# State-space B and C rows: from selection matmuls into PSUM to DMA out of DRAM into an SBUF ring

## The chip, the core and the metric

The kernel runs on one NeuronCore of one Trainium2 chip. The metric is the device time of one launch in microseconds (us). The names of the engines are those of the profile: PE is TensorE, DVE is VectorE, ACT is ScalarE, POOL is GpSimd, SP is the engine that issues the DMAs.

## What is computed

The network has six layers on 4 sequences of 512 tokens and 128 features, each with normalisation and a residual: a routed feed-forward attention ("ffn"), a 16-head attention ("mha"), the ffn again, a mixture of experts ("moe"), a state-space block ("mamba"), and the moe again. The change touches only the state-space block. Its core in the reference is

```python
x_dbl = x @ W_x                      # 96 columns: 64 for dt, 16 for B, 16 for C
dt = softplus(x_dbl[..., :64] @ W_dt + b_dt)
Bm = x_dbl[..., 64:80]
Cm = x_dbl[..., 80:]
def step(h, inp):
    dA = exp(dt_t[..., None] * A)
    h = dA * h + (dt_t * x_t)[..., None] * B_t[:, None, :]
    y = einsum('bdn,bn->bd', h, C_t)
```

with 256 inner channels d, 16 states n, 512 steps t. For each state n the recurrence over t is one scan for every channel. B and C depend on n and t and not on the channel, so the same row of 512 numbers is needed on all 128 partitions.

## The kernel before

**Units.** The program loops twice (`Fori(0, PAIRS)`) over two sequences at a time. In a pass the five engines walk through 12 units, `UNITS`: each layer for sequence 0 and then for sequence 1. So the state-space unit runs four times, twice in each pass. Every engine has its own instruction stream written out by hand, with explicit semaphore waits; nothing reorders it. While an engine works through a unit it also takes pieces ("stages") of the next unit's normalisation and routing, by the tables `DVE_STAGES`, `POOL_STAGES`, `ACT_STAGES` and `PE_STAGES` (L72 to L76), through `hand_over`, after the state with that number.

**Ahead of the states.** PE forms x_dbl for 512 tokens in PSUM bank 4, rows 0 to 63 for dt, rows 64 to 95 for B and C (L1513). ACT copies the dt rows (L815) and the B and C rows as bf16 (L816). DVE and POOL split the remainder into two more bf16 parts (L1158 to L1162 and L609), so that `n_bc` has the B and C rows three times, in 96 partitions, with a sum that is exact to float32. In the meantime PE, ACT, DVE and POOL compute dt as a guarded softplus on tiles of 128x1024 (two halves of the channels), L1167 to L1178 on DVE with L613 and L615 on POOL beside it.

**The loop over the states.** Per state n, for the two halves m of the channels:

- PE spreads row n of B over 128 partitions into bank 4 or 5 with one bf16 matmul against a selection matrix `pick` (L1527), and row n of C into bank 0 or 1 (L1531).
- ACT forms `n_da` = exp(dt * A) for each half (L831) and copies the C bank to SBUF, `n_cs` (L835).
- DVE multiplies dt*x by the B bank, `n_db` (L1186, one input in SBUF, one in PSUM), twice, and then runs the two scans `n_h` (L1194, both inputs in SBUF).
- POOL multiplies `n_h` by `n_cs` into `n_hc` (L623, both inputs in SBUF), twice.
- PE adds `n_hc` to the output in banks 2 and 3 by a float32 matmul against the identity (L1536).

`n_db`, `n_da`, `n_h` and `n_hc` exist once per half, so: the product of state n+1 waits for the scan of state n of its half, the scan of n+1 waits for POOL's product of n, and POOL's product of n+1 waits for PE.

```python
n_dbs.by(V.tensor_tensor(n_db[:, m, :], n_dtx[:, m, :], bank[:, 4 + n % 2, :], ALU.mult))
n_scan.by(V.tensor_tensor_scan(n_h[:, m, :], n_da[:, m, :], n_db[:, m, :], 0.0, ALU.mult, ALU.add))
n_hcs.by(nc.gpsimd.tensor_tensor(n_hc[:, m, :], n_h[:, m, :], n_cs[:, n // 2 % 2, :], ALU.mult))
```

After the last state DVE adds the skip term (L1202), gates (L1204), PE multiplies by W_out (L1542, 8 calls) and DVE adds the residual (L991).

**SP's stream** has the loads at the start, the expert weights, the attention's transfers over DRAM (`stack_dram`, `max_dram`), and the input and output of the pass. In the state-space units it has nothing to do.

## Time and profile before

| | |
|---|---|
| Time, median of 3 runs (us) | 1673.01 |
| Lowest and highest (us) | 1671.74, 1675.35 |
| Span of the profiled execution (us) | 1673.0 |
| PE busy | 1308.8 us, 78% |
| DVE busy | 1126.0 us, 67% |
| ACT busy | 685.1 us, 41% |
| POOL busy | 493.3 us, 29% |
| DMA moved | 33.11 MB, mean 20 GB/s |

The span is that of one execution taken by the profiler; it agrees with the median of the other runs within 0.1 us. Busy times are means over stages with different limits; the four state-space units lie at 522 to 636, 636 to 751, 1345 to 1458 and 1458 to 1573 us of the span. In a timeline, an instruction that the engine has begun but that cannot go on counts as busy. Two equal instructions that follow each other are merged, "x2". A float32 matmul shows as two records.

### The profile page before, as it was taken

To read this page: it belongs to the slowest core of one execution; us is meant where nothing else is said; L and a number is where in the kernel's file an instruction comes from. 1 tells how busy PE (TensorE), PEld (TensorE's weight loads), DVE (VectorE), ACT (ScalarE), POOL (GpSimd) and SP (SyncE) were. 2 spreads that over 40 slices of the span, in tenths; PEclk is the share of its full clock that TensorE was granted. 3 is DMA by queue.
4 is the path that set the end of the run, shared out by engine and by line. 5 is a ranking of instruction groups with operands and counts; after the bars stand their busy time and mean duration, and the time that the engine had idled before them with its cause. 6 is when DMAs were issued, how large, how long until landed. Compare 5 with 4: busy or idle time off the path is not lost.

```text
span 1673.0 us, 17199 instructions
## 1 busy us (share of the span) xinstructions
PE 1308.8 (78%) x5912; PEld 799.2 (48%) x5912; DVE 1126.0 (67%) x1997; ACT 685.1 (41%) x1136; POOL 493.3 (29%) x349
## 2 busy tenths in 40 slices
PE   0997768898977575669969967679988957747698
PEld 0675334576654122227636744336766622212366
DVE  5666655445775997987646665545556769889765
ACT  4443434343435344424425415253444443344244
POOL 2001000000644573646410010000016536547365
PEclk9998979899998677869979979799999977877899
DMA  5203030000000000000002020200000000000000
GB/s 204 57 14 88 4 89 3 1 1 1 1 1 0 1 0 0 1 1 1 13 33 70 19 71 22 70 3 1 1 1 1 1 0 1 0 1 0 1 1 19
DMA packets 23401, 33.11 MB, mean 20 GB/s; under 512 B 2992, under 2 KB 19152, under 8 KB 22864
## 3 DMA queue, kind: packets, MB, share of 16 engines
q1 hardware_dynamic: 23312, 31.99, 6.6%
q8 instruction: 48, 0.79, 0.2%
q14 instruction: 41, 0.34, 0.1%
HBM read 24.44 MB, written 8.06 MB: 19 GB/s over the span
## 4 chain that ended last, share of the span: by engine, by line
PE 47%; DVE 31%; issue 9%; DMA 5%; ACT 5%; POOL 1%; SPq 1%; POOLq 0%; DVEq 0%; ACTq 0%
PE bank L1227 10%; PE bank L1229 10%; PE bank L1228 10%; DVE n_h L1194 6%; DVE n_db L1186 4%; DVE a_mx L1132 3%; PE bank L1300 3%; PE bank L1236 2%; PE bank L1446 2%; DMA X<-in_x_dram 2%; PE bank L1486 2%; PE bank L1354 2%; DMA a_k<-stack_dram 2%; PE bank L1427 2%; DVE m_t L1057 1%
## 5 line engine op out<-in xcount | busy, mean ns | idle before, releaser
L590 POOL TENSOR_TENSOR m_hhl<-m_h,m_hhh 128x512 fp32r<-128x512 f32 x144 | 186.3, 1297 | 272.0 <-ACT m_hhh L755 271.7
L1536 PE MATMUL bank<-n_hc,ident 128*128 128x512 f32 x256 | 191.5, 861 | 83.1 <-POOL n_hc L623 79.8
L623 POOL TENSOR_TENSOR n_hc<-n_h,n_cs 128x512 f32<-128x512 f32 x128 | 210.4, 1662 | 128.9 <-DVE n_h L1194 123.7
L997 DVE SCALAR_TENSOR_TENSOR f_hl<-bank,f_hh 128x512 fp32r<-128x512 f32 x192 | 132.1, 690 | 128.1 <-ACT f_hh L695 127.0
L566 POOL TENSOR_TENSOR small<-small,half 128x4 f32<-128x4 f32 x24 | 24.3, 1012 | 600.3 <-DVE small L900 599.2
L695 ACT ACTIVATE f_hh<-bank 128x512 fp32r<-128x512 f32 x192 | 114.7, 597 | 207.1 <-PE bank L1300 206.7
L1194 DVE TENSOR_TENSOR_SCAN n_h<-n_da,n_db 128x512 f32<-128x512 f32 x128 | 192.0, 1538 | 3.4 <-POOL n_hc L623 2.3
L831 ACT ACTIVATE n_da<-n_dt,amat 128x512 f32<-128x512 f32 x128 | 91.7, 721 | 187.4 <-DVE n_h L1194 167.5
L1057 DVE TENSOR_TENSOR m_t<-m_sl,bank 128x512 f32<-128x512 f32 x128 | 87.8, 686 | 96.0 <-PE bank L1229 82.1
L1536 PEld LDWEIGHTS bank<-n_hc,ident 128*128 128x128 f32 x256 | 52.8, 241 | 187.0 <-POOL n_hc L623 177.1
L1132 DVE TENSOR_REDUCE a_mx<-bank 128x1 f32<-128x384 f32 (+3 forms) x176 | 105.9, 639 | 47.5 <-PE bank L1488 46.5
L1227 PE MATMUL bank<-xT_h,mw_h 128*128 128x512 f32 x288 | 123.7, 429 | 17.6 <-DVE m_t L1057 13.2
L749 ACT ACTIVATE m_sl<-bank 128x512 f32<-128x512 f32 x144 | 85.7, 596 | 120.4 <-PE bank L1229 118.3
L770 ACT ACTIVATE a_p<-bank 128x1024 f32<-128x1024 f32 (+3 forms) x128 | 86.9, 700 | 97.5 <-PE bank L1429 96.3
L755 ACT ACTIVATE m_hhh<-m_h 128x512 fp32r<-128x512 f32 x144 | 90.3, 627 | 68.0 <-DVE m_h L1060 48.8
L1228 PE MATMUL bank<-xT_l,mw_h 128*128 128x512 f32 x288 | 117.3, 407 | 0.0
L1229 PE MATMUL bank<-xT_h,mw_l 128*128 128x512 f32 x288 | 117.2, 407 | 0.0
L1227 PE MATMUL bank<-f_hh,fw_h 128*128 128x512 f32 x192 | 109.6, 571 | 6.0 <-DVE f_hl L997 6.0
L1486 PE MATMUL bank<-a_k,a_q 128*128 128x128 bf16 (+3 forms) x256 | 77.2, 350 | 30.2 <-DMA a_k<-stack_dram 18.8
L1060 DVE TENSOR_TENSOR m_h<-m_t,bank 128x512 f32<-128x512 f32 x128 | 88.0, 687 | 4.4
L1227 PE MATMUL bank<-xT_h,fw_h 128*128 128x512 f32 x192 | 86.5, 450 | 3.5 <-DVE R L936 1.9
L1186 DVE TENSOR_TENSOR n_db<-n_dtx,bank 128x512 f32<-128x512 f32 x128 | 80.8, 670 | 0.2
(247 smaller groups left out, 2820.4 us busy)
## 6 DMA issues: line engine op xcount, KB each, us to landing
w_stage<-in_mw_dram SPq DMA_DIRECT2D x16, 384.0 KB, 3.2
a_q<-stack_dram SPq DMA_DIRECT2D x8, 512.0 KB, 5.6
a_k<-stack_dram SPq DMA_DIRECT2D x16, 256.0 KB, 7.7
stage_fw<-in_fw_dram SPq DMA_DIRECT2D x2, 1536.0 KB, 10.0
stack_dram<-R SPq DMA_DIRECT2D x16, 192.0 KB, 2.8
stack_dram<-R SPq DMA_DIRECT2D x16, 128.0 KB, 2.5
stage_b<-in_bias_dram SPq DMA_DIRECT2D x1, 1728.0 KB, 10.2
X<-in_x_dram SPq DMA_DIRECT2D x5, 256.0 KB, 2.8
```

The lines of the kernel that those rows point to most:

```text
L590: m_lo.by(nc.gpsimd.tensor_tensor(m_hh[1][:, i % 3, :], m_h[:, i % 3, :], m_hh[0][:, i % 3, :].bitcast(F32), ALU.subtract))
L623: n_hcs.by(nc.gpsimd.tensor_tensor(n_hc[:, m, :], n_h[:, m, :], n_cs[:, n // 2 % 2, :], ALU.mult))
L695: f_hi.by(act.activation(f_h[0][:, i % 4, :], bank[:, i % 3, :], ACT.Relu))
L997: f_lo.by(V.scalar_tensor_tensor(f_h[1][:, i % 4, :], bank[:, i % 3, :], 0.0, f_h[0][:, i % 4, :].bitcast(F32), ALU.max, ALU.subtract))
L1132: a_m1.by(V.tensor_reduce(a_mx[:, quad, qt, h0:h0 + nh], src, AX_X, ALU.max, negate=True))
L1186: n_dbs.by(V.tensor_tensor(n_db[:, m, :], n_dtx[:, m, :], bank[:, 4 + n % 2, :], ALU.mult))
L1194: n_scan.by(V.tensor_tensor_scan(n_h[:, m, :], n_da[:, m, :], n_db[:, m, :], 0.0, ALU.mult, ALU.add))
L1227: mm(dst, w[0], x[0], start=start, stop=False)
L1228: mm(dst, w[0], x[1], start=False, stop=False)
L1229: return mm(dst, w[1], x[0], start=False, stop=stop)
L1486: mm(bank[:, b, c * w:(c + 1) * w], a_q[:, h // 2, qt * P:(qt + 1) * P], a_k[:, h, 0:w], start=True, stop=False)
L1536: n_ya.by(mm(bank[:, 2 + m, :], ident[:], n_hc[:, m, :], start=n == 2, stop=n == NSTATE + 1))
```

## The change

ACT copies all 96 rows of x_dbl to SBUF as float32, `n_xd`, in one instruction. SP writes the 32 rows of B and C to a DRAM tensor, `state_dram`, and waits for that. Then it loads for each state the two rows, B and C, with a source whose partition step is 0, so that each of the 128 partitions gets both: 512 KB a load, into a ring of three slots, `n_row`. A load into a slot waits until the products and POOL's multiplications that read the slot three states earlier are done. DVE's product and POOL's multiplication read `n_row` in place of the PSUM bank and `n_cs`. The selection matmuls, the copies of C, the split into three bf16 parts on ACT, DVE and POOL, and their semaphores go. `n_low` gets a buffer of its own.

```diff
--- before.py
+++ after.py
@@ -22,7 +22,7 @@
 EXPERTS, MLPS = 8, 9
 MSTEPS = MLPS * 2
 HEADS, DH, SLOTS = 16, 8, 6
-NSTATE, NHALF = 16, 2
+NSTATE, NHALF, ROWS = 16, 2, 3
 EPS = 1e-5
 LEAF_SCALE = float(np.float32(1.0) / np.sqrt(P).astype(np.float32))
 HEAD_SCALE = float(1.0 / np.sqrt(np.float32(DH)))
@@ -259,24 +259,23 @@
         n_xp = sb("n_xp", [P, NHALF, T + 4], F32, s)
         n_xc = sb("n_xc", [P, NHALF, T], F32, s)
         n_sz = sb("n_sz", [P, NHALF, T], F32, s)
-        n_dtr = sb("n_dtr", [64, T], F32, s)
+        n_xd = sb("n_xd", [96, T], F32, s)
         n_dt = sb("n_dt", [P, NHALF, T], F32, s)
         n_dtx = sb("n_dtx", [P, NHALF, T], F32, s)
         n_da = sb("n_da", [P, NHALF, T], F32, s)
         n_db = sb("n_db", [P, NHALF, T], F32, s)
         n_h = sb("n_h", [P, NHALF, T], F32, s)
         n_hc = sb("n_hc", [P, NHALF, T], F32, s)
-        n_cs = sb("n_cs", [P, 2, T], F32, s)
-        n_bc = sb("n_bc", [96, T], BF16, s)
-        n_r = sb("n_r", [96, T], F32, s)
-        n_mid = sb("n_mid", [96, T], BF16, s)
+        n_low = sb("n_low", [P, 2, T], F32, s)
+        n_row = sb("n_row", [P, ROWS, 2, T], F32, s)
         s.close()
         n_cv = n_cor = n_hc
-        n_abs, n_u, n_ln, n_low, n_pos = n_db, n_h, n_da, n_cs, n_dtx
+        n_abs, n_u, n_ln, n_pos = n_db, n_h, n_da, n_dtx
 
 
         stack_dram = nc.dram_tensor("stack_dram", [2, 2, P // 2, HEADS // 2, T], BF16, kind="Internal").ap()
         max_dram = nc.dram_tensor("max_dram", [QUADS, 12, T], BF16, kind="Internal").ap()
+        state_dram = nc.dram_tensor("state_dram", [2, 2, NSTATE, T], F32, kind="Internal").ap()
 
 
         signals = []
@@ -393,10 +392,8 @@
         n_sil = sig("n_sil", "mamba", 4)
         n_xdb = sig("n_xdb", "mamba", 1)
         n_dtc = sig("n_dtc", "mamba", 1)
-        n_bc1 = sig("n_bc1", "mamba", 1)
-        n_bcp = sig("n_bcp", "mamba", 1)
-        n_mids = sig("n_mids", "mamba", 1)
-        n_bcm = sig("n_bcm", "mamba", 1)
+        n_bcw = sig("n_bcw", "mamba", 1, 16)
+        n_bcl = [sig(f"n_bcl_{r}", "mamba", len(range(r, NSTATE, ROWS)), 16) for r in range(ROWS)]
         n_dtp = sig("n_dtp", "mamba", 2)
         n_abss = sig("n_abss", "mamba", 2)
         n_us = sig("n_us", "mamba", 1)
@@ -406,10 +403,7 @@
         n_poss = sig("n_poss", "mamba", 2)
         n_dts = sig("n_dts", "mamba", 1)
         n_dtxs = sig("n_dtxs", "mamba", 1)
-        n_br = sig("n_br", "mamba", NSTATE)
-        n_cr = sig("n_cr", "mamba", NSTATE)
         n_das = sig("n_das", "mamba", 2 * NSTATE)
-        n_csc = sig("n_csc", "mamba", NSTATE)
         n_dbs = sig("n_dbs", "mamba", 2 * NSTATE)
         n_scan = sig("n_scan", "mamba", 2 * NSTATE)
         n_hcs = sig("n_hcs", "mamba", 2 * NSTATE)
@@ -437,6 +431,9 @@
             else:
 
                 eng.wait_ge(pair_done, j + 1)
+
+        def row_in(eng, k, n):
+            eng.wait_ge(n_bcl[n % ROWS].sem, n_bcl[n % ROWS].at(k, n // ROWS))
 
         def job_bank(i):
 
@@ -511,6 +508,16 @@
                                 r = 64 * odd + MAX_ROW
                                 a_mld[quad].by(sp.dma_start(a_q[r:r + 3, 2 * quad:2 * quad + 2],
                                                       max_dram[quad].rearrange("(c h o) t -> o c h t", c=3, o=2)[odd]))
+                    if kind == "mamba":
+                        sp.wait_ge(n_dtc.sem, n_dtc.at(k, 0))
+                        n_bcw.by(sp.dma_start(state_dram[p].rearrange("c n t -> (c n) t"), n_xd[64:96]))
+                        sp.wait_ge(n_bcw.sem, n_bcw.at(k, 0))
+                        for n in range(NSTATE):
+                            if n >= ROWS:
+                                sp.wait_ge(n_dbs.sem, n_dbs.at(k, 2 * (n - ROWS) + 1))
+                                sp.wait_ge(n_hcs.sem, n_hcs.at(k, 2 * (n - ROWS) + 1))
+                            n_bcl[n % ROWS].by(sp.dma_start(
+                                n_row[:, n % ROWS], state_dram[p, :, n].unsqueeze(0).to_broadcast([P, 2, T])))
                     if u + 1 < NU and UNITS[u + 1][0] == "mha":
                         k = kth[u + 1]
                         if k == 0:
@@ -605,10 +612,6 @@
                     if kind == "mamba":
                         n_fill.by(nc.gpsimd.memset(n_xp[:, :, 0:3], 0.0))
 
-                        pool.wait_ge(n_mids.sem, n_mids.at(k, 0))
-                        n_bcm.by(nc.gpsimd.tensor_copy(n_bc[32:64], n_mid[64:96]))
-
-                        pool.wait_ge(n_bcm.sem, n_bcm.at(k, 0))
                         pool.wait_ge(n_us.sem, n_us.at(k, 0))
                         n_a1.by(nc.gpsimd.tensor_scalar(n_low[:], n_u[:], -0.5, 1.0, ALU.mult, ALU.add))
                         pool.wait_ge(n_a1.sem, n_a1.at(k, 0))
@@ -617,10 +620,10 @@
                             m = n % 2
 
                             pool.wait_ge(n_scan.sem, n_scan.at(k, n))
-                            pool.wait_ge(n_csc.sem, n_csc.at(k, n // 2))
+                            row_in(pool, k, n // 2)
                             if n >= 2:
                                 pool.wait_ge(n_ya.sem, n_ya.at(k, n - 2))
-                            n_hcs.by(nc.gpsimd.tensor_tensor(n_hc[:, m, :], n_h[:, m, :], n_cs[:, n // 2 % 2, :],
+                            n_hcs.by(nc.gpsimd.tensor_tensor(n_hc[:, m, :], n_h[:, m, :], n_row[:, n // 2 % ROWS, 1],
                                                              ALU.mult))
                             if m == 1:
                                 hand_over(u, n // 2)
@@ -812,8 +815,7 @@
 
                 act.activation(preload, half[:, 0, 0:NT], ACT.Exp)
                 act.wait_ge(n_xdb.sem, n_xdb.at(k, 0))
-                n_dtc.by(act.activation(n_dtr[:], bank[0:64, 4, :], ACT.Copy))
-                n_bc1.by(act.activation(n_bc[64:96], bank[64:96, 4, :], ACT.Copy))
+                n_dtc.by(act.activation(n_xd[:], bank[0:96, 4, :], ACT.Copy))
                 for m in range(2):
                     act.wait_ge(n_dtp.sem, n_dtp.at(k, m))
                     n_abss.by(act.activation(n_abs[:, m, :], bank[:, m, :], ACT.Abs, bias=b_dt[:, m:m + 1]))
@@ -829,10 +831,6 @@
                         if n >= 1:
                             act.wait_ge(n_scan.sem, n_scan.at(k, 2 * n + m - 2))
                         n_das.by(act.activation(n_da[:, m, :], n_dt[:, m, :], ACT.Exp, scale=amat[:, m, n:n + 1]))
-                    act.wait_ge(n_cr.sem, n_cr.at(k, n))
-                    if n >= 2:
-                        act.wait_ge(n_hcs.sem, n_hcs.at(k, 2 * n - 3))
-                    n_csc.by(act.activation(n_cs[:, n % 2, :], bank[:, n % 2, :], ACT.Copy))
                     hand_over(j, u, n)
 
             def hand_over(j, u, i):
@@ -1154,14 +1152,6 @@
                         step(j, ins)
                 n_cvs.by(ins)
 
-                dve.wait_ge(n_bc1.sem, n_bc1.at(k, 0))
-                step(j, V.tensor_tensor(n_r[64:96], bank[64:96, 4, :], n_bc[64:96], ALU.subtract))
-                n_mids.by(V.tensor_copy(n_mid[64:96], n_r[64:96]))
-                dve.wait_ge(n_mids.sem, n_mids.at(k, 0))
-                step(j, V.tensor_tensor(n_r[64:96], n_r[64:96], n_mid[64:96], ALU.subtract))
-                n_bcp.by(V.tensor_copy(n_bc[0:32], n_r[64:96]))
-
-
                 dve.wait_ge(n_us.sem, n_us.at(k, 0))
                 dve.wait_ge(n_sil.sem, n_sil.at(k, 3))
                 step(j, V.tensor_scalar(n_cor[:], n_u[:], 1.0, -1.0, ALU.add, ALU.add))
@@ -1178,12 +1168,13 @@
                 n_dtxs.by(V.tensor_tensor(n_dtx[:], n_dt[:], n_xc[:], ALU.mult))
                 dve.wait_ge(n_dtxs.sem, n_dtxs.at(k, 0))
                 for n in range(NSTATE):
-                    dve.wait_ge(n_br.sem, n_br.at(k, n))
+                    row_in(dve, k, n)
                     for m in range(NHALF):
                         i = 2 * n + m
                         if n >= 1:
                             dve.wait_ge(n_scan.sem, n_scan.at(k, i - 2))
-                        n_dbs.by(V.tensor_tensor(n_db[:, m, :], n_dtx[:, m, :], bank[:, 4 + n % 2, :], ALU.mult))
+                        n_dbs.by(V.tensor_tensor(n_db[:, m, :], n_dtx[:, m, :], n_row[:, n % ROWS, 0],
+                                                 ALU.mult))
                     for m in range(NHALF):
                         i = 2 * n + m
                         dve.wait_ge(n_dbs.sem, n_dbs.at(k, i))
@@ -1514,22 +1505,9 @@
                 n_xdb.by(ins)
                 pe.wait_ge(n_dtc.sem, n_dtc.at(k, 0))
                 for m in range(2):
-                    n_dtp.by(mm(bank[:, m, :], wdt[:, m, :], n_dtr[:], start=True, stop=True))
-
-                pe.wait_ge(n_bcp.sem, n_bcp.at(k, 0))
-                pe.wait_ge(n_bcm.sem, n_bcm.at(k, 0))
-                pe.wait_ge(n_poss.sem, n_poss.at(k, 1))
-                pe.wait_ge(n_abss.sem, n_abss.at(k, 1))
+                    n_dtp.by(mm(bank[:, m, :], wdt[:, m, :], n_xd[0:64], start=True, stop=True))
+
                 for n in range(NSTATE + 2):
-                    if n < NSTATE:
-                        if n >= 2:
-                            pe.wait_ge(n_dbs.sem, n_dbs.at(k, 2 * n - 3))
-                        n_br.by(mm(bank[:, 4 + n % 2, :], pick[:, n:n + 1].to_broadcast([96, P]), n_bc[:],
-                                   start=True, stop=True))
-                        if n >= 2:
-                            pe.wait_ge(n_csc.sem, n_csc.at(k, n - 2))
-                        n_cr.by(mm(bank[:, n % 2, :], pick[:, 16 + n:17 + n].to_broadcast([96, P]), n_bc[:],
-                                   start=True, stop=True))
                     if n >= 2:
                         for m in range(2):
                             pe.wait_ge(n_hcs.sem, n_hcs.at(k, 2 * n - 4 + m))
```

What moves, as the streams show it. PE, from the dt projection (`n_dtr`, `n_xd`) into the loop over the states, before:

```order
L1517 MATMUL bank<-n_dtr,wdt 128x512 [waits n_dtc]
L1517 MATMUL bank<-n_dtr,wdt 128x512
L1527 MATMUL bank<-n_bc,pick 128x512 [waits n_poss,n_abss,n_bcm,n_bcp]
L1531 MATMUL bank<-n_bc,pick 128x512
L1527 MATMUL bank<-n_bc,pick 128x512
L1531 MATMUL bank<-n_bc,pick 128x512
L1527 MATMUL bank<-n_bc,pick 128x512 [waits n_dbs]
L1531 MATMUL bank<-n_bc,pick 128x512 [waits n_csc]
L1536 MATMUL bank<-n_hc,ident 128x512 [waits n_hcs] x2
L1527 MATMUL bank<-n_bc,pick 128x512 [waits n_dbs]
```

and in the changed kernel, where the rows `n_hc` run on until the next unit's transposes (`R`), with the rest of the loop and the output product behind them:

```order
L1508 MATMUL bank<-n_xd,wdt 128x512 [waits n_dtc]
L1508 MATMUL bank<-n_xd,wdt 128x512
L1514 MATMUL bank<-n_hc,ident 128x512 [waits n_hcs] x10
L1227 MATMUL bank<-ident,R 128x128 [waits g_xn]
L1227 MATMUL bank<-ident,R 128x128 x3
L1514 MATMUL bank<-n_hc,ident 128x512 [waits n_hcs] x22
L1520 MATMUL bank<-wout,n_db 128x128 [waits n_y]
```

The two matmuls of each state and the first wait for four signals are gone; only the accumulations stay.

DVE, from the end of the softplus to the second state, before:

```order
L1178 TENSOR_TENSOR n_dtx<-n_dt,n_xc 128x1024 [waits n_sil,n_dts]
L1186 TENSOR_TENSOR n_db<-n_dtx,bank 128x512 [waits n_br,n_dtxs]
L1186 TENSOR_TENSOR n_db<-n_dtx,bank 128x512
L1194 SCALAR_TENSOR_TENSOR n_h<-n_da,n_db 128x512 [waits n_das,n_dbs] x2
L885 BN_STATS st<-X 128x6 x4
L888 BN_AGGR mv<-st 128x2 [waits dve_step]
L888 BN_AGGR mv<-st 128x2 x3
L900 TENSOR_SCALAR small<-mv 128x4 [waits dve_step]
L1186 TENSOR_TENSOR n_db<-n_dtx,bank 128x512 [waits n_scan,n_br]
```

and now:

```order
L1168 TENSOR_TENSOR n_dtx<-n_dt,n_xc 128x1024 [waits n_sil,n_dts]
L1176 TENSOR_TENSOR n_db<-n_dtx,n_row 128x512 [waits n_bcl_0,n_dtxs]
L1176 TENSOR_TENSOR n_db<-n_dtx,n_row 128x512
L1185 SCALAR_TENSOR_TENSOR n_h<-n_da,n_db 128x512 [waits n_das,n_dbs] x2
L883 BN_STATS st<-X 128x6 x4
L886 BN_AGGR mv<-st 128x2 [waits dve_step]
L886 BN_AGGR mv<-st 128x2 x3
L898 TENSOR_SCALAR small<-mv 128x4 [waits dve_step]
L1176 TENSOR_TENSOR n_db<-n_dtx,n_row 128x512 [waits n_scan,n_bcl_1]
```

The order is the same. The product's second input is `n_row` and not the bank, and it waits for a load (`n_bcl`) and not for PE (`n_br`). ACT's stream loses the second copy and the copy of C in each state.

SP, which went from the attention's last transfers to the output of the pass, has in between for each of the two units:

```order
L509 DMA a_q<-max_dram 3x2x512 [waits a_mwr]
L509 DMA a_q<-max_dram 3x2x512
L513 DMA state_dram<-n_xd 32x512 [waits n_dtc]
L519 DMA n_row<-state_dram 128x2x512 [waits n_bcw]
L519 DMA n_row<-state_dram 128x2x512 x2
L519 DMA n_row<-state_dram 128x2x512 [waits n_hcs,n_dbs] x13
L513 DMA state_dram<-n_xd 32x512 [waits n_dtc]
```

Each unit adds one write and 16 loads, 13 of which wait for DVE and POOL.

## Rows read from the trace of the kernel before

**Rows 1.** The page: span, and part 4, the chain that ended last, by engine

```profile
span 1673.0 us, 17199 instructions
...
PE 47%; DVE 31%; issue 9%; DMA 5%; ACT 5%; POOL 1%; SPq 1%; POOLq 0%; DVEq 0%; ACTq 0%
```

**Rows 2.** Windows: start:end, length, busy us of PE, PEld, DVE, ACT, POOL, then granted clock

```profile
548.00:629.00 81.00, 56.94 (x93) 16.85 (x94) 78.77 (x102) 30.18 (x48) 54.53 (x34) 0.72 0.00 0
629.00:636.00 7.00, 4.29 (x21) 2.46 (x20) 3.74 (x6) 0.00 (x0) 0.97 (x2) 1.00 0.00 0
...
743.00:751.00 8.00, 4.25 (x20) 3.75 (x19) 3.54 (x6) 0.00 (x0) 0.00 (x0) 0.50 0.00 0
```

**Rows 3.** Timeline of two steady states: start us, length us, engine, line, operation, [idle before]

```profile
604.11 3.33 POOL L623 TENSOR_TENSOR n_hc<-n_h,n_cs 128x512 f32<-128x512 f32 x2 [1.16 <-DVE n_h L1194]
...
605.07 1.25 DVE L1186 TENSOR_TENSOR n_db<-n_dtx,bank 128x512 f32<-128x512 f32 x2
...
606.27 3.02 PE L1536 MATMUL bank<-n_hc,ident 128*128 128x512 f32 x4 [1.71 <-POOL n_hc L623]
606.35 3.29 DVE L1194 TENSOR_TENSOR_SCAN n_h<-n_da,n_db 128x512 f32<-128x512 f32 x2
...
608.60 3.33 POOL L623 TENSOR_TENSOR n_hc<-n_h,n_cs 128x512 f32<-128x512 f32 x2 [1.16 <-DVE n_h L1194]
```

**Rows 4.** Instructions by tile, min/median/max ns: the scan (tile n_h)

```profile
L1194 DVE TENSOR_TENSOR_SCAN n_h<-n_da,n_db x128: 1191/1211/2230, 549.4 to 1558.4; 128x512 f32<-128x512 f32 x128
```

**Rows 5.** The same view for tile n_db: PSUM-fed and SBUF-fed products

```profile
L1186 DVE TENSOR_TENSOR n_db<-n_dtx,bank x128: 654/673/689, 548.1 to 1556.7; 128x512 f32<-128x512 f32 x128
...
L1204 DVE TENSOR_TENSOR n_db<-n_db,n_sz x8: 691/692/694, 630.7 to 1568.1; 128x512 f32<-128x512 f32 x8
```

**Rows 6.** Timeline ahead of the first state: VectorE beside GpSimd

```profile
538.80 3.20 POOL L615 TENSOR_TENSOR n_cs<-n_cs,n_h 128x1024 f32<-128x1024 f32 x1
...
539.82 3.25 DVE L1170 TENSOR_TENSOR n_hc<-n_hc,n_da 128x1024 f32<-128x1024 f32 x1
...
543.11 1.22 DVE L1172 TENSOR_TENSOR n_hc<-n_hc,n_cs 128x1024 f32<-128x1024 f32 x1
```

**Rows 7.** Timeline of GpSimd alone, first unit of the first pass

```profile
581.65 3.33 POOL L623 TENSOR_TENSOR n_hc<-n_h,n_cs 128x512 f32<-128x512 f32 x2 [3.74 <-DVE n_h L1194]
...
626.55 3.31 POOL L623 TENSOR_TENSOR n_hc<-n_h,n_cs 128x512 f32<-128x512 f32 x2 [1.16 <-DVE n_h L1194]
```

**Rows 8.** The same view, second unit of the first pass

```profile
693.31 3.33 POOL L623 TENSOR_TENSOR n_hc<-n_h,n_cs 128x512 f32<-128x512 f32 x2 [1.16 <-DVE n_h L1194]
699.10 1.27 POOL L623 TENSOR_TENSOR n_hc<-n_h,n_cs 128x512 f32<-128x512 f32 x1 [2.45 <-PE bank L1536]
...
707.93 3.32 POOL L623 TENSOR_TENSOR n_hc<-n_h,n_cs 128x512 f32<-128x512 f32 x2 [1.50 <-DVE n_h L1194]
```

**Rows 9.** Timeline of VectorE alone: a four-element product beside GpSimd

```profile
561.84 1.16 DVE L878 TENSOR_TENSOR small<-small 128x4 f32<-128x4 f32 x1
```

**Rows 10.** DMA issues, KB each, median us to landing

```profile
a_q<-stack_dram SPq DMA_DIRECT2D x8, 512.0 KB, 5.6
...
rope<-in_rope_dram SPq DMA_DIRECT2D x2, 512.0 KB, 4.2
stack_dram<-R SPq DMA_DIRECT2D x16, 64.0 KB, 2.1
```

**Rows 11.** Timeline of PE: output product of the first unit

```profile
632.84 2.05 PE L1542 MATMUL bank<-wout,n_db 128*128 128x128 f32 x16 [1.80 <-DVE n_db L1204]
```

**Rows 12.** Timeline: output product of the second unit

```profile
746.76 3.78 PE L1542 MATMUL bank<-wout,n_db 128*128 128x128 f32 x16 [3.28 <-DVE n_db L1204]
```

**Rows 13.** Timeline ahead of the first state: who waits for what

```profile
534.45 0.69 ACT L819 ACTIVATE n_db<-bank,col 128x512 f32<-128x512 f32 x1 [0.60 <-PE bank L1517]
...
537.12 0.69 DVE L1167 TENSOR_SCALAR n_hc<-n_h 128x1024 f32<-128x1024 f32 x1 [0.63 <-ACT n_h L821]
...
540.87 0.58 PE L1527 MATMUL bank<-n_bc,pick 96*128 96x512 bf16 x1 [5.59 <-ACT n_dtx L825]
```

## The prediction

> **What bounds the kernel now.** The page's chain first: PE holds 47% and DVE 31% of it [rows 1]. That is a mean over unlike units, and the change lies in four of them, so the window view comes next. In the 81 us loop over the states of one unit DVE is busy for 78.8 us, POOL for 54.5, PE for 56.9, ACT for 30.2 [rows 2]. PE and ACT have room, and DVE looks full. It is not full of work, though. In the timeline of a steady state [rows 3] POOL takes up its two products at 604.11, ends at 607.44 (604.11 + 3.33) and takes up the next two at 608.60: a state costs 4.49 us. DVE takes up its two scans at 606.35 and ends at 609.64 (606.35 + 3.29). A scan takes 1.2 us in the median [rows 4], two 2.4, so about 0.9 of the 3.29 is waiting. What ends there is POOL's second product, at 607.44: from then to 609.64 are 2.20 us, both scans without a gap. POOL shows the mirror image: its 3.33 us begin while the second scan runs, and 4.49 - 2.20 leaves 2.29 us in which it works. So **a state is 2.20 us of scans plus 2.29 us of POOL's products, one after the other and never together**, although the semaphores would let them overlap.
>
> The same pair shows it ahead of the loop [rows 6]. A product of DVE over 128x1024 with both inputs in SBUF takes 1.22 us with POOL idle (at 543.11). The one at 539.82 takes 3.25 us; POOL's product began at 538.80 and ends at 542.00, and DVE is done 1.07 us after that. The op with one input in PSUM knows no such thing: 128 products `n_db` last 654 to 689 ns [rows 5], and the pair taken up at 605.07 is over in 1.25 us in the middle of POOL's 3.33 us [rows 3]. It is the one piece of DVE's loop that is hidden, inside POOL's 2.29 us.
>
> **The change part by part.**
>
> *The product's input moves from PSUM to SBUF.* By itself this costs nothing: a product of the same shape with two SBUF inputs takes 691 ns against 673 [rows 5]. But now it is of the kind that does not run beside POOL's products. The pair costs 1.2 us when the two follow each other (1.25 less the 0.65 of the second is 0.60 from start to start). Does it find another place to hide? No: it needs the previous scan of its half, the next scan needs it, and all else in the cycle is scans and POOL's products, which it can't share. The cover is gone, and 4.49 becomes up to 5.69.
>
> I take a little off. An instruction that has queued shows less time after its release: 1.07 against 1.22 [rows 6]. POOL and DVE will now take turns more often (at 561.84 a tiny DVE product waits 1.16 us, POOL's first product, and gets in ahead of the second [rows 9]), so some of the fixed part hides. Bounds for a period: 0.9 (two queued products with 0.15 off each, and as much for POOL's second), and 1.4 (two products of 0.69 in full). I take **+1.1 us**, nearest the pair as rows 3 show it, less 0.1.
>
> *How many periods pay.* After some states DVE does a piece of the next unit's work, long enough for POOL to be finished before the next product; there the product is already on the path, and nothing is lost. From 581.65 to 626.55 are ten periods, 44.90 us, 4.49 each [rows 7]; with two more of that length nearer the start it is 12 of the 15. In the second unit, with more routing work, it is again 12 of 15, three of which take 14.62 us in place of 13.47 because PE is late once (POOL waits 2.45 us for it) [rows 8]. So 24 periods a pass, 48 in all: 48 x 1.1 = **+52.8 us**.
>
> *PE loses two matmuls a state.* PE isn't what a state waits for, so this pays only at that late spot: 1.15 us in a pass, **-2** for both.
>
> *ACT loses a copy a state* (it is busy for 30 of 81 us [rows 2]): 0. *Ahead of the loop* the second copy on ACT goes, but ACT then waited 0.60 us for PE anyway; the split on DVE goes, but DVE then waited 0.63 us for ACT; the first selection matmul was ready at 540.87, 7 us before the loop [rows 13]. POOL's small copy lay before the same signal of ACT. All 0; the softplus chain hides them and is untouched.
>
> *The DMAs.* SP is idle in these units, so nothing is queued behind its new waits but its own next loads. First rows: the copy is done before ACT's next instruction at 534.45 [rows 13], the write of 64 KB lands in 2.1 us, a load of 512 KB in 4.2 to 5.6 [rows 10]: 542 at the latest, against a first need at 548 [rows 2]. In the loop a slot is released by POOL's last product of state n and needed by the product of n+3. By the new cycle that leaves two periods less a part of one: about 9.4 us, against 5.6. Cost 0; the cover is those 4 us. No load here reads one row for 128 partitions, so 4.2 is no firm floor; were it 12 us, see below. 64 loads of 512 KB are 33.5 MB, and 512 KB per 5.6 us is 94 GB/s.
>
> *Clock.* With fewer matmuls PE's granted clock may sit differently at the ends of the units. The output product takes 2.05 us in a stretch granted 1.00 and 3.78 in one granted 0.50 (2.4 and 1.2 GHz) [rows 2, 11, 12]: per unit -1.7 or +1.7, and perhaps as much again in what follows. I take 0, with -4 to +8 for the range.
>
> Sum, against the profiled execution's 1673.0 us (the median is 1673.01): 1673 + 52.8 - 2 = **1724 us**.
>
> **A rule that reads otherwise.** The rows show one-input DVE products untouched and two-input ones stretched beside POOL [rows 5, 6]. The Trainium skill, page "SBUF — State Buffer", section "Who interferes with whom", says that a DVE instruction with two SBUF inputs contends with a GpSimd instruction that reads SBUF, and that whoever comes second is blocked in full; by that rule, the trace agrees. The Trainium skill's page "Advanced Engine Details and Errata", section "VectorE Performance Modes", names only DVE's two-port modes as in conflict with GpSimd, and its page "VectorE: DVE Perf Modes" (section "Why tensor_tensor can't do 2×_2P or 4×") denies a two-tensor product such a mode; by those alone the change would cost nothing, which is the first rival below.
>
> **The rivals.**
>
> *The new product runs beside POOL all the same.* Then the cover stays, and only PE's late spot is gained: 1673 - 2 = 1671 us, no change that can be measured (about 0.2%, 3.3 us, is what these runs can tell), or with a kinder clock just faster. For it: only scans and 1024-wide products were seen to wait. Against it: the tiny product of rows 9 is the same operation and waited. It decides if the products keep 0.65 us beside POOL. 4%.
>
> *Part of it hides.* If DVE's queued products slip into gaps of POOL's issue, 0.5 to 0.8 us a period stay: 48 x 0.65 = 31, less 2: 1702 us. Against it: 2.20 and 2.29 already fill 4.49. 8%.
>
> *Each turn costs more.* Every change of holder adds 0.1 us, and the products last their full 0.69: 1.5 a period, 72 - 2: 1743 us. For it: there will be up to twice as many changes. 14%.
>
> *The rows come late.* If a load takes longer than 9.4 us, three periods together take that latency plus about 7.3 us. At 12 us a state takes 6.4, another 0.8 in some 50 periods: 1764 us. For it: 128 reads of the same DRAM row have no example here. Against it: 5.6 us was with other transfers in flight. 5%.
>
> **How the numbers follow.** The forecast has 69%. Its own range: 0.9 to 1.3 a period is 43 to 62 us, less 2, with the clock's -4 to +8: 1710 to 1741. To leave out no more than 2 in 10 I go down to 1704, with some of the part that hides, and up to 1750, with the costlier turns. Slower by over 0.2%: the forecast and the last three rivals, 96%, less 2 for the unforeseen: 94%. The first rival's 4% and those 2 are shared between within 0.2%, 3%, and faster, 3%.
>
> **What would show it.** In the changed profile: the DVE product shows up to 1.8 us (its own 0.6 behind one of POOL's 1.1 to 1.2) and not 0.67 in steady states; a steady period is 5.5 to 5.7 us; scans and POOL's products keep 2.20 and 2.29 us of work; the loop of the first unit is 12 x 1.1 = 13 us longer, while the periods with DVE's other work keep their length; DVE waits nowhere for `n_bcl`; a load lands in 4 to 6 us; everything outside the four units keeps its time. Wrong: products of 0.67 us in a 4.49 us period, waits for the loads, or a period far from 5.6.

## The result, and the profile after

| | before | after |
|---|---|---|
| Time, median of 4 runs each (us) | 1673.49 | **1720.53** |
| Lowest and highest (us) | 1671.74, 1675.35 | 1718.41, 1724.84 |
| Span of the profiled execution (us) | 1673.0 | 1716.6 |
| DMA moved (MB) | 33.11 | 66.93 |

The changed kernel takes 1.0288 times as long (95% interval 1.0266 to 1.0309), 47 us more. The page of the changed kernel: its span, the chain by engine and by line, and the groups of the loop (busy time, mean ns of one, idle before):

```profile
span 1716.6 us, 16857 instructions
...
PE 46%; DVE 33%; issue 9%; DMA 5%; ACT 4%; POOL 1%; SPq 1%; POOLq 0%; DVEq 0%; ACTq 0%
PE bank L1218 10%; PE bank L1220 9%; PE bank L1219 9%; DVE n_db L1176 7%; DVE n_h L1185 5%; DVE a_mx L1130 3%; PE bank L1227 2%; PE bank L1437 2%; PE bank L1291 2%; DMA X<-in_x_dram 2%; PE bank L1477 2%; PE bank L1345 2%; DMA a_k<-stack_dram 2%; PE bank L1418 2%; DVE m_t L1055 1%
...
L626 POOL TENSOR_TENSOR n_hc<-n_h,n_row 128x512 f32<-128x512 f32 x128 | 233.6, 1844 | 153.4 <-DVE n_h L1185 141.8
...
L1176 DVE TENSOR_TENSOR n_db<-n_dtx,n_row 128x512 f32<-128x512 f32 x128 | 176.7, 1419 | 0.2
...
L1185 DVE TENSOR_TENSOR_SCAN n_h<-n_da,n_db 128x512 f32<-128x512 f32 x128 | 151.1, 1220 | 0.0
```

DVE's share of the chain went from 31% to 33% [rows 1], and the product, `n_db` L1176, holds more of it (7%) than the scan (5%). The group line of the product says what happened: 176.7 us busy, 1419 ns a piece, for an instruction that needs 0.69 us. POOL's product stands at 1844 ns, where the page before had 1662. The view by tile, ns min/median/max, for scan, product and POOL's product:

```profile
L1185 DVE TENSOR_TENSOR_SCAN n_h<-n_da,n_db x128: 1191/1206/2280, 544.6 to 1603.3; 128x512 f32<-128x512 f32 x128
L626 POOL TENSOR_TENSOR n_hc<-n_h,n_row x128: 1254/1752/2102, 545.9 to 1605.5; 128x512 f32<-128x512 f32 x128
...
L1176 DVE TENSOR_TENSOR n_db<-n_dtx,n_row x128: 660/1687/1751, 543.4 to 1601.6; 128x512 f32<-128x512 f32 x128
```

The product was at 654 to 689 ns before [rows 5]; its median is now 1687. The scan's maximum, 2280 ns, is near what it was [rows 4], but its mean on the page is 1220 ns, where it was 1538: it waits hardly any more. The timeline of two steady states, to be laid beside [rows 3]:

```profile
601.16 3.77 POOL L626 TENSOR_TENSOR n_hc<-n_h,n_row 128x512 f32<-128x512 f32 x2 [1.76 <-DVE n_h L1185]
602.12 3.35 DVE L1176 TENSOR_TENSOR n_db<-n_dtx,n_row 128x512 f32<-128x512 f32 x2
...
603.31 3.55 PE L1514 MATMUL bank<-n_hc,ident 128*128 128x512 f32 x4 [1.96 <-POOL n_hc L626]
...
605.39 2.33 DVE L1185 TENSOR_TENSOR_SCAN n_h<-n_da,n_db 128x512 f32<-128x512 f32 x2
...
606.68 3.77 POOL L626 TENSOR_TENSOR n_hc<-n_h,n_row 128x512 f32<-128x512 f32 x2 [1.76 <-DVE n_h L1185]
607.64 3.36 DVE L1176 TENSOR_TENSOR n_db<-n_dtx,n_row 128x512 f32<-128x512 f32 x2
```

A state is 606.68 - 601.16 = **5.52 us**, 4.49 before. The order in it: POOL's first product (from 601.16, taken singly it ends at 603.25), DVE's first product behind it (ends at 603.80), POOL's second (604.92), DVE's second (605.47), and then both scans from 605.39 in 2.33 us, with POOL idle until 606.68. DVE takes the product up at 602.12 and ends it at 605.47; before, the same pair ended in 1.25 us in the middle of POOL's. POOL's 3.33 became 3.77. PE's additions lie inside it and hold up nothing. POOL alone, over the first unit, and at the place in the second where PE was late:

```profile
545.94 3.33 POOL L626 TENSOR_TENSOR n_hc<-n_h,n_row 128x512 f32<-128x512 f32 x2 [8.66 <-DVE n_h L1185]
...
551.70 3.77 POOL L626 TENSOR_TENSOR n_hc<-n_h,n_row 128x512 f32<-128x512 f32 x2 [0.95 <-DVE n_h L1185]
...
579.04 3.76 POOL L626 TENSOR_TENSOR n_hc<-n_h,n_row 128x512 f32<-128x512 f32 x2 [3.75 <-DVE n_h L1185]
...
634.33 3.31 POOL L626 TENSOR_TENSOR n_hc<-n_h,n_row 128x512 f32<-128x512 f32 x2 [1.76 <-PE bank L1514]
...
709.98 3.77 POOL L626 TENSOR_TENSOR n_hc<-n_h,n_row 128x512 f32<-128x512 f32 x2 [1.76 <-DVE n_h L1185]
716.47 3.47 POOL L626 TENSOR_TENSOR n_hc<-n_h,n_row 128x512 f32<-128x512 f32 x2 [2.71 <-PE bank L1514]
721.10 3.76 POOL L626 TENSOR_TENSOR n_hc<-n_h,n_row 128x512 f32<-128x512 f32 x2 [1.16 <-DVE n_h L1185]
```

From 579.04 to 634.33 are ten periods, 55.29 us where they were 44.90 [rows 7]. In the second unit the two periods about PE's late spot take 721.10 - 709.98 = 11.12, twice 5.56: its extra time is gone [rows 8], though POOL still waits 2.71 us for PE there (row 716.47). The period behind that wait is short, 721.10 - 716.47 = 4.63: while POOL waits, DVE's first product has nothing to queue behind and takes 0.66 us. The loads, KB each and median us to landing, beside the write:

```profile
n_row<-state_dram SPq DMA_DIRECT2D x64, 512.0 KB, 4.8
...
state_dram<-n_xd SPq DMA_DIRECT2D x4, 64.0 KB, 1.6
```

A load takes 4.8 us in the median (4.6 to 9.0), and no wait of DVE or POOL for one is in the trace. The windows of the loop and of its end (length, busy us of PE, PEld, DVE, ACT, POOL, granted clock, DMA share, GB/s), and the output product of the first unit:

```profile
548.00:634.00 86.00, 53.13 (x64) 14.97 (x64) 85.52 (x91) 20.78 (x29) 55.90 (x32) 0.60 0.35 80
636.50:646.00 9.50, 7.12 (x21) 4.32 (x21) 3.59 (x6) 0.00 (x0) 1.20 (x2) 0.54 0.00 0
```

```profile
641.34 3.79 PE L1520 MATMUL bank<-wout,n_db 128*128 128x128 f32 x16 [1.57 <-DVE n_db L1195]
```

PE is busy for 53 of 86 us, at a granted clock of 0.60 where it was 0.72 [rows 2], and the output product takes 3.79 us, nearly all at 1.2 GHz, where it took 2.05 at 2.4 GHz [rows 11].

**Where the 47 us are.** The table has the four units of the two profiled executions in pieces: from the last addition to X to the first product `n_db`; the loop, from POOL's first pair to its last; and from that last pair to the next addition to X (us). The piece between the first two, from the first product to POOL's first pair, is 2.50 or 2.51 everywhere.

| Unit | ahead, before | ahead, now | loop, before | loop, now | end, before | end, now | whole, before | whole, now |
|---|---|---|---|---|---|---|---|---|
| 1 | 25.62 | 25.60 | 75.90 | 88.39 | 8.38 | 10.84 | 112.4 | 127.3 |
| 2 | 24.07 | 26.31 | 73.97 | 85.39 | 14.29 | 14.02 | 114.8 | 128.2 |
| 3 | 25.51 | 24.08 | 75.91 | 88.40 | 8.38 | 10.62 | 112.3 | 125.6 |
| 4 | 24.07 | 24.07 | 73.50 | 85.37 | 14.06 | 13.92 | 114.1 | 125.9 |

The units took 453.7 us together and take 507.1 now: 53.4 us more. The loops have 48.3 of that: 48 periods of 1.04 are 49.9, and PE's late spots, 1.15 us in the first pass and 0.67 in the second, fall to 0.1 together, which gives back 1.7. The other 5.1 us lie outside the loops and go with PE's clock. The ends of units 1 and 3 are 2.5 and 2.2 us longer. The start of unit 2 is 2.2 us longer, in a stretch granted 0.81 (645.9 to 659.2) where it was granted 0.99 (635.7 to 649.0). The start of unit 3 is 1.4 us shorter, granted 0.97 where it was 0.88. Small gains at the ends of units 2 and 4 make up the rest.

The rest of the program, which the change does not touch, took 9.8 us less in this profiled execution. That part differs from run to run of all kernels here: it is 1209.6 to 1219.4 us in the nine profiled executions, with the changed kernel at the low end and the kernel before at the high one. I count it as spread between executions; why these two lie at its ends was not settled.

### The profile page after: what moved, and what is told of

It is laid out like the page before. It is cut to its first block, busy times and chain, and to the rows that moved or that the text cites. A ratio compares the mean times of both kernels' runs of the same rounds, so it can differ in the third digit from the quotient of the medians.

```text
span 1716.6 us, 16857 instructions
## 1 busy us (share of the span) xinstructions
PE 1292.3 (75%) x5734; PEld 792.3 (46%) x5784; DVE 1167.7 (68%) x1981; ACT 651.5 (38%) x1068; POOL 512.8 (30%) x345
## 2 busy tenths in 40 slices
DMA packets 41002, 66.93 MB, mean 39 GB/s; under 512 B 4081, under 2 KB 20241, under 8 KB 40465
## 4 chain that ended last, share of the span: by engine, by line
PE 46%; DVE 33%; issue 9%; DMA 5%; ACT 4%; POOL 1%; SPq 1%; POOLq 0%; DVEq 0%; ACTq 0%
PE bank L1218 10%; PE bank L1220 9%; PE bank L1219 9%; DVE n_db L1176 7%; DVE n_h L1185 5%; DVE a_mx L1130 3%; PE bank L1227 2%; PE bank L1437 2%; PE bank L1291 2%; DMA X<-in_x_dram 2%; PE bank L1477 2%; PE bank L1345 2%; DMA a_k<-stack_dram 2%; PE bank L1418 2%; DVE m_t L1055 1%
## 5 line engine op out<-in xcount | busy, mean ns | idle before, releaser
L1514 PE MATMUL bank<-n_hc,ident 128*128 128x512 f32 x256 | 220.9, 994 | 199.7 <-POOL n_hc L626 199.5
L626 POOL TENSOR_TENSOR n_hc<-n_h,n_row 128x512 f32<-128x512 f32 x128 | 233.6, 1844 | 153.4 <-DVE n_h L1185 141.8
L1514 PEld LDWEIGHTS bank<-n_hc,ident 128*128 128x128 f32 x256 | 60.1, 281 | 350.4 <-POOL n_hc L626 344.8
L1176 DVE TENSOR_TENSOR n_db<-n_dtx,n_row 128x512 f32<-128x512 f32 x128 | 176.7, 1419 | 0.2
L1185 DVE TENSOR_TENSOR_SCAN n_h<-n_da,n_db 128x512 f32<-128x512 f32 x128 | 151.1, 1220 | 0.0
L1477 PE MATMUL bank<-a_k,a_q 128*128 128x128 bf16 (+3 forms) x244 | 72.8, 348 | 28.4 <-DMA a_k<-stack_dram 16.9
```

The lines of the kernel that those rows point to most:

```text
L1176: n_dbs.by(V.tensor_tensor(n_db[:, m, :], n_dtx[:, m, :], n_row[:, n % ROWS, 0], ALU.mult))
L1477: mm(bank[:, b, c * w:(c + 1) * w], a_q[:, h // 2, qt * P:(qt + 1) * P], a_k[:, h, 0:w], start=True, stop=False)
L1514: n_ya.by(mm(bank[:, 2 + m, :], ident[:], n_hc[:, m, :], start=n == 2, stop=n == NSTATE + 1))
```

## The experiments

**The theories.** *Exclusion*: a DVE instruction with two SBUF inputs and a POOL product never run together; the product in the loop became such an instruction when its B row moved to SBUF, and that alone costs the 47 us. *Rivals*: (a) DMA traffic into SBUF, or waits for it, slows the loop; (b) the C row from the ring, the removed copies or the lower PE clock are the cause. Each kernel is the changed one with one thing moved or put back. Seven kernels ran, each in three rounds, with the kernel before beside it (1669.9 us for the first four, 1671.5 us for the last three); every ratio is to that.

**B by matmul again, C from the ring.** The loads carry C alone, 256 KB. The split into three bf16 parts is back with the selection matmuls of B; the cut shows the two lines that matter.

```diff
+                        n_br.by(mm(bank[:, 4 + n % 2, :], pick[:, n:n + 1].to_broadcast([96, P]), n_bc[:],
...
-                        n_dbs.by(V.tensor_tensor(n_db[:, m, :], n_dtx[:, m, :], n_row[:, n % ROWS, 0],
+                        n_dbs.by(V.tensor_tensor(n_db[:, m, :], n_dtx[:, m, :], bank[:, 4 + n % 2, :],
```

> B comes by selection matmul into PSUM again, C stays in the DMA ring (loads of 256 KB). Theory (DVE instructions with two SBUF inputs and POOL's products take turns, and the product of dt*x and B has become one): the DVE product is back at 0.67 us, a steady state at 4.49 us, the time at that of the kernel before, 1668 to 1678 us. Rival (the loads into SBUF, or waits for them, slow DVE or POOL): half the traffic stays, so about half of the loss, 1690 to 1705 us.

Measured: 1669.0 us (before beside it 1669.9), ratio 0.9989 (0.9972 to 1.0006). The whole loss is gone, with C still from DRAM. Its timeline:

```profile
602.97 3.33 POOL L639 TENSOR_TENSOR n_hc<-n_h,n_row 128x512 f32<-128x512 f32 x2 [1.16 <-DVE n_h L1206]
603.93 1.25 DVE L1197 TENSOR_TENSOR n_db<-n_dtx,bank 128x512 f32<-128x512 f32 x2
...
607.46 3.33 POOL L639 TENSOR_TENSOR n_hc<-n_h,n_row 128x512 f32<-128x512 f32 x2 [1.16 <-DVE n_h L1206]
```

The product is at 1.25 us, the period at 607.46 - 602.97 = 4.49, as in [rows 3].

**C by matmul and ACT's copy again, B from the ring.** The selection matmuls of C and the split are back too; the loads carry B alone.

```diff
+                    n_csc.by(act.activation(n_cs[:, n % 2, :], bank[:, n % 2, :], ACT.Copy))
...
-                            n_hcs.by(nc.gpsimd.tensor_tensor(n_hc[:, m, :], n_h[:, m, :], n_row[:, n // 2 % ROWS, 1],
+                            n_hcs.by(nc.gpsimd.tensor_tensor(n_hc[:, m, :], n_h[:, m, :], n_cs[:, n // 2 % 2, :],
```

> C comes by selection matmul and ACT copy again, B stays in the DMA ring (loads of 256 KB). Theory: the product still has two SBUF inputs, so a steady state stays at 5.5 us and the time at 1714 to 1728 us although half the DMA traffic is gone. Rival (traffic): 1690 to 1705 us.

Measured: 1721.92 us, ratio 1.03 (1.0272 to 1.0327), as slow as the change. The timeline:

```profile
601.74 3.77 POOL L641 TENSOR_TENSOR n_hc<-n_h,n_cs 128x512 f32<-128x512 f32 x2 [1.76 <-DVE n_h L1212]
...
607.27 3.76 POOL L641 TENSOR_TENSOR n_hc<-n_h,n_cs 128x512 f32<-128x512 f32 x2 [1.76 <-DVE n_h L1212]
608.23 3.35 DVE L1203 TENSOR_TENSOR n_db<-n_dtx,n_row 128x512 f32<-128x512 f32 x2
```

607.27 - 601.74 = 5.53, and half of the loads' bytes are gone. The loss is that of the B row, not of C, its copies or the amount of traffic. These two runs still move B in both its place and its way of getting there; the next holds the way fixed.

**Everything from the ring, dt*x in PSUM.** Banks 4 and 5 are free in the changed kernel, so `n_dtx` can lie there: the product keeps its DMA-fed row and gets a PSUM input from the other side.

```diff
         n_abs, n_u, n_ln, n_pos = n_db, n_h, n_da, n_dtx
+        n_dtx = bank[:, 4:6, :]
```

> The changed kernel with one edit: dt*x, the product's first input, lives in PSUM banks 4 and 5; all loads stay at 512 KB. Theory: one SBUF input, so no turn-taking for it: 0.67 us a product, 4.49 us a steady state, 1665 to 1676 us. Rival (traffic, or late rows): as the changed kernel, 1715 to 1725 us.

Measured: 1669.69 us, ratio 1.0002 (0.9991 to 1.0013). With the same loads, no wait for them and the same missing matmuls as in the change, one address takes back the whole loss (a ratio of 1.0288). In the profiled execution the four units take 453.7 us again:

```profile
602.19 3.33 POOL L627 TENSOR_TENSOR n_hc<-n_h,n_row 128x512 f32<-128x512 f32 x2 [1.16 <-DVE n_h L1186]
603.15 1.26 DVE L1177 TENSOR_TENSOR n_db<-bank,n_row 128x512 f32<-128x512 f32 x2
...
606.68 3.33 POOL L627 TENSOR_TENSOR n_hc<-n_h,n_row 128x512 f32<-128x512 f32 x2 [1.16 <-DVE n_h L1186]
```

This is the run that settles it: by either rival nothing that matters has changed, and it should have stayed at about 1720.

It shows one thing more, on PE's late spot in the second unit. PE has lost its two matmuls a state here as well, yet with the period back at 4.49 us the late spot is there again:

```profile
688.09 3.33 POOL L627 TENSOR_TENSOR n_hc<-n_h,n_row 128x512 f32<-128x512 f32 x2 [1.16 <-DVE n_h L1186]
694.57 1.26 POOL L627 TENSOR_TENSOR n_hc<-n_h,n_row 128x512 f32<-128x512 f32 x1 [3.15 <-PE bank L1515]
...
703.39 3.32 POOL L627 TENSOR_TENSOR n_hc<-n_h,n_row 128x512 f32<-128x512 f32 x2 [1.50 <-DVE n_h L1186]
```

The three periods take 703.39 - 688.09 = 15.30 us, more than the 14.62 of [rows 8]; those of the second pass take 14.16. So it is not PE's shorter stream that rids the changed kernel of this time, but the longer period.

**The scan's coefficients in PSUM as well.** If two SBUF inputs are the whole matter, scans should leave POOL alone too once `n_da` is in banks 0 and 1.

```diff
+        n_dtx = bank[:, 4:6, :]
...
-                        n_das.by(act.activation(n_da[:, m, :], n_dt[:, m, :], ACT.Exp, scale=amat[:, m, n:n + 1]))
+                        n_das.by(act.activation(bank[:, m, :], n_dt[:, m, :], ACT.Exp, scale=amat[:, m, n:n + 1]))
...
-                        n_scan.by(V.tensor_tensor_scan(n_h[:, m, :], n_da[:, m, :], n_db[:, m, :], 0.0,
+                        n_scan.by(V.tensor_tensor_scan(n_h[:, m, :], bank[:, m, :], n_db[:, m, :], 0.0,
```

> As e3, and exp(dt*A) goes to PSUM banks 0 and 1, so that the scans too have one SBUF input. Theory: nothing of DVE in the loop waits for POOL any more; a steady state is DVE's own 2 x 0.6 + 2 x 1.12 = 3.45 us, or PE's 3.8 where its clock is at half; 48 periods x 0.7 to 1.0 us less than 4.49: 1622 to 1640 us. Rival (the scans wait for POOL's result by their semaphores and not for the port): 4.49 stays, 1665 to 1676 us.

Measured: **1612.48 us**, ratio 0.9658 (0.9626 to 0.969), 10 us under the range. Timeline and tiles:

```profile
603.19 2.49 POOL L627 TENSOR_TENSOR n_hc<-n_h,n_row 128x512 f32<-128x512 f32 x2 [1.30 <-DVE n_h L1186]
604.14 1.27 DVE L1177 TENSOR_TENSOR n_db<-bank,n_row 128x512 f32<-128x512 f32 x2
...
605.32 2.33 DVE L1186 TENSOR_TENSOR_SCAN n_h<-bank,n_db 128x512 f32<-128x512 f32 x2
...
606.62 2.49 POOL L627 TENSOR_TENSOR n_hc<-n_h,n_row 128x512 f32<-128x512 f32 x2 [0.93 <-DVE n_h L1186]
```

```profile
L1186 DVE TENSOR_TENSOR_SCAN n_h<-bank,n_db x128: 1192/1208/1224, 546.7 to 1498.9; 128x512 f32<-128x512 f32 x128
L627 POOL TENSOR_TENSOR n_hc<-n_h,n_row x128: 1260/1265/1445, 548.0 to 1500.3; 128x512 f32<-128x512 f32 x128
```

No scan takes over 1224 ns any more (2230 before [rows 4]), POOL's pair takes 2.49 in place of 3.33, and a state is 606.62 - 603.19 = 3.43 us. DVE goes from products to scans to products with no gap: now it is full of work and the bound. 48 periods at 1.06 less than before's 4.49 are 51 us, and 1669.9 - 51 = 1619. The four units are 55.4 us shorter (398.3), all of it in the loops: the periods that the expectation left out, those with DVE's other work, shrink too (in the first unit 5.74 to 4.91 and 9.23 to 8.42). The slack of the loads shrinks with the period, and DVE waits for one once, 0.3 us.

**The scan's coefficients alone in PSUM.** Here the product is the one that excludes, and the scan is free.

```diff
-                        n_das.by(act.activation(n_da[:, m, :], n_dt[:, m, :], ACT.Exp, scale=amat[:, m, n:n + 1]))
+                        n_das.by(act.activation(bank[:, m, :], n_dt[:, m, :], ACT.Exp, scale=amat[:, m, n:n + 1]))
...
-                        n_scan.by(V.tensor_tensor_scan(n_h[:, m, :], n_da[:, m, :], n_db[:, m, :], 0.0,
+                        n_scan.by(V.tensor_tensor_scan(n_h[:, m, :], bank[:, m, :], n_db[:, m, :], 0.0,
```

> The changed kernel with exp(dt*A) in PSUM banks 0 and 1: the scans have one SBUF input, the products of dt*x and B keep two. Theory: POOL's first product runs beside the second scan, then product, POOL's second, product take turns as in the changed kernel; a steady state is 2 x 1.12 of scans and about 2.5 of turns, 4.6 to 4.9 us, so the time lies 30 to 45 us under the changed kernel's 1720: 1675 to 1692 us. Rival (only the products matter, the scans never waited for the port but for POOL's signals): 5.5 us a state, 1715 to 1725 us.

Measured: 1671.12 us, ratio 0.9996 (0.998 to 1.0011), 4 us under the range.

```profile
603.00 2.93 POOL L626 TENSOR_TENSOR n_hc<-n_h,n_row 128x512 f32<-128x512 f32 x2 [1.76 <-DVE n_h L1185]
603.96 2.52 DVE L1176 TENSOR_TENSOR n_db<-n_dtx,n_row 128x512 f32<-128x512 f32 x2
...
606.41 2.32 DVE L1185 TENSOR_TENSOR_SCAN n_h<-bank,n_db 128x512 f32<-128x512 f32 x2
...
607.70 2.93 POOL L626 TENSOR_TENSOR n_hc<-n_h,n_row 128x512 f32<-128x512 f32 x2 [1.76 <-DVE n_h L1185]
```

The period, 607.70 - 603.00 = 4.70, is inside what was expected; the time is lower than the range. The trace shows where. The expectation counted 48 periods, but the other periods of a unit shrink by as much (5.76, 9.22 and 7.06 to 4.92, 8.39 and 6.23 in the first unit): the loops are 48.9 us shorter than in the changed kernel, not 40. And the ends of the units are 5.5 us shorter, with the output product of the first back at 2.05 us. The pair of products takes 2.52 us beside POOL, the scans 2.32: cheaper than the change by 0.83 a period, since only DVE's short instructions are held up. That it ties with the kernel before, by another route, is chance.

**The softplus correction in PSUM too.** The same rule ahead of the loop: `n_cor` goes to banks 4 and 5, on top of the edit before last.

```diff
-        n_cv = n_cor = n_hc
+        n_cv, n_cor = n_hc, bank[:, 4:6, :]
```

> As e4, and the softplus correction that DVE builds ahead of the first state lives in PSUM banks 4 and 5 until dt*x takes them. Theory: the 128x1024 instructions that lasted 1.94 and 3.25 us beside POOL are back at about 1.25 us, and what is left on the path is POOL's own two instructions; 2 us a unit, 8 us in all less than e4: 1601 to 1608 us. Rival (they wait for ACT's or POOL's signals anyway): 1612 us as e4.

Measured: **1600.24 us**, ratio 0.9577 (0.955 to 0.9603), the fastest here and 1 us under the range. The timeline ahead of the first state, to be laid beside [rows 6]:

```profile
534.10 1.23 DVE L1158 TENSOR_SCALAR bank<-n_h 128x1024 f32<-128x1024 f32 x1 [9.28 <-ACT n_h L824]
...
535.29 2.36 POOL L619 TENSOR_TENSOR n_low<-n_low,n_h 128x1024 f32<-128x1024 f32 x1
535.36 1.23 DVE L1159 TENSOR_TENSOR bank<-n_h,bank 128x1024 f32<-128x1024 f32 x1
...
536.63 1.23 DVE L1161 TENSOR_TENSOR bank<-bank,n_da 128x1024 f32<-128x1024 f32 x1
...
542.95 1.29 DVE L1177 TENSOR_TENSOR n_db<-bank,n_row 128x512 f32<-128x512 f32 x2
```

The product of 3.25 us is now 1.23 (the one ahead of it, 1.94 us before, is 1.23 too), and POOL's beside it 2.36 for 3.20. The first instruction, a tensor_scalar that now writes PSUM, takes 1.23 where it took 0.69: a price of 0.54. From its start to the first product are 8.85 us, 11.03 in the run without this edit: 2.18 a unit, 8.7 in all. The medians are 12.2 us apart. The ends of the units are 3.5 us shorter than there in the profiled executions, which fits the clock: the output product of the first takes 2.05 us here, 3.62 there. No run holds the clock fixed, so that part is argued.

**A ring of two slots.** It probes the slack of the loads. In the changed kernel that slack can be read off the trace: a load goes out at 605.00, behind POOL's second product of state n, for the product of state n+3. The products of n+1 are under way by then, those of n+2 are taken up at 607.64 and those of n+3 at 613.17, so 8.2 us are at hand.

```diff
-NSTATE, NHALF, ROWS = 16, 2, 3
+NSTATE, NHALF, ROWS = 16, 2, 2
```

> The changed kernel with two slots in the ring in place of three. The row of state n+2 is loaded once POOL is done with state n; by the changed kernel's steady state some 3.9 us then pass before DVE wants it, against a landing time of 4.8 us. Theory (three slots cover the load, two do not): DVE waits up to 1 us a state for the row, POOL's second product goes ahead meanwhile, a state costs 5.5 to 5.9 us: 1720 to 1740 us. Rival (late rows are part of the loss already with three slots, and each slot less costs a whole landing time a state): over 1800 us.

Measured: 1727.95 us, ratio 1.0348 (1.0318 to 1.0379). The timeline, and DVE's waits (us in total, times, longest):

```profile
604.40 3.33 POOL L626 TENSOR_TENSOR n_hc<-n_h,n_row 128x512 f32<-128x512 f32 x2 [2.36 <-DVE n_h L1185]
...
607.23 1.65 DVE L1176 TENSOR_TENSOR n_db<-n_dtx,n_row 128x512 f32<-128x512 f32 x2 [1.79 <-DMA n_row<-state_dram]
...
608.80 2.33 DVE L1185 TENSOR_TENSOR_SCAN n_h<-n_da,n_db 128x512 f32<-128x512 f32 x2
```

```profile
DVE n_db L1176 <- DMA n_row<-state_dram: 65.3, 43, 2.5
```

The time is inside the range, but the waits are longer than the "up to 1 us" that was expected: 1.79 us here, 2.5 at most. With two slots a row asked for at 605.00 would be needed at 607.64, after 2.6 us and not the 3.9 of the expectation, against 4.8 to landing. Yet 43 waits, 65.3 us of them, cost only some 7 us more than the change: while DVE waits, POOL works alone, and the products (median 685 ns in this run) then find it done. The wait takes the place of the exclusion and not a place beside it. Three slots are enough at 5.5 us a state; with two a steady period is 5.69 us.

## Why the prediction was right

The time predicted was 1724, with 1710 to 1741 for the forecast itself; measured 1720.53. Step by step:

- **A state is scans plus POOL's products, never together.** Right. Beyond the trace, a run shows it: with one operand of the scan in PSUM as well, POOL's pair falls to 2.49 and the scans to 2.33 for two, and the period with them.
- **The product loses its cover.** Right, and shown to be the cause of the whole loss: 1669.69 with one operand in PSUM, 1720.53 without. It shows "up to 1.8 us", as foretold: 1687 ns in the median, 1751 at most.
- **+1.1 us a period.** Measured 5.53 - 4.49 = 1.04; 0.06 a period, or 2.9 us of the sum, too much. The order of events was the one assumed: the products slip in behind each of POOL's two, as the tiny product did in [rows 9], and part of each one's fixed time hides.
- **48 periods.** The count holds, though one reading behind it does not. In the first unit ten periods go from 4.49 to 5.53, as the row of POOL above shows, but only one more of 4.49 us lies nearer the start, and not two. The twelfth is made up by two periods of 5.18 and 6.36 us that become 5.53 and 7.06. Two periods with more of DVE's other work kept their length (5.76 from 545.94 to 551.70, 5.74 before; 9.22 about a state with more routing work, 9.23 before).
- **PE's late spot, -2.** The number holds (1.7), by luck: the reason does not. The prediction gave it to PE's two lost matmuls. The run with `n_dtx` in PSUM has lost them too, and its late spot is still there (15.30 and 14.16 us for three periods, against 13.47 without one), while in the changed kernel POOL still waits 2.71 us for PE. What took the time off the path is the longer period, in which POOL's wait for PE takes the place of a product's wait for POOL. The second pass also had less to give than the first, 0.67 us and not 1.15.
- **Clock 0, between -4 and +8.** It was +5.1, inside the bounds; the middle was too low. The end of the first unit is 2.5 us longer, 1.74 of it the output product, as the bound had it, and so is the end of the third (2.2). The start of the second is 2.2 longer, that of the third 1.4 shorter. In the loop of the first unit PE has fewer matmuls and longer pauses between them, at a granted clock of 0.60, and comes out of it at the lower level.
- **DMAs, 0.** Right in the cost: 4.8 us to landing where up to 5.6 was allowed. The slack was taken too large, though: 8.2 us were at hand, not about 9.4, since the first product of a state is taken up 2.8 us before POOL ends the pair beside it. The two-slot ring shows that the third slot's cover was real: without it DVE waits 43 times.
- **All else ahead of the loop, 0.** Right: from the addition to X to the first product are 25.6 us in the first unit of both, and 24.07 in the fourth; what units 2 and 3 differ by goes with the clock.

The measured terms sum to 49.9 - 1.7 + 5.1 = 53.3 us, which is what the units of the profiled executions bear out (53.4), and would give 1726. The medians differ by 47.0 only. The untouched code took 9.8 us less in the profiled executions, about what the same code differs by from one execution to another; whether the change has a share in that stays open. So the terms are right to 3 us each, the clock's to 5. That the median came out below 1724, and not above it as these terms have it, goes with the untouched part and not with the prediction.

Of the rivals, the first (the product keeps 0.65 us beside POOL) falls on the median of 1687 ns; the one where part hides (0.65 a period) and the costlier turns (1.5) on the 1.04; the late rows on the absence of any wait for them. The Trainium skill, page "SBUF — State Buffer", section "Who interferes with whom", describes two SBUF inputs against GpSimd as the case that excludes, and at most one as the case that does not; by that rule, the runs agree, on either side of the product and for the scan. That whoever comes second is blocked in full, as the prediction has it from that page, holds but for some 0.4 us of 3.74 a state (last section). The Trainium skill's page "Advanced Engine Details and Errata", section "VectorE Performance Modes", read alone, would have given 1671; the measurement decides against that reading.
